# Gain and bias of the layer norm in two scalar_tensor_tensor operations on VectorE, and one weight load counted apart

## The reference, cut to what matters

```python
h = gelu(x @ W_down[role] + b_down[role])        # 512 -> 256
u = h @ W_up[role] + b_up[role]                  # 256 -> 512
y = x + u
mean = y.mean(-1); var = ((y - mean) ** 2).mean(-1)
out = (y - mean) * rsqrt(var + 1e-5) * gamma[role] + beta[role]
```

## Time and profile before

| | before |
|---|---|
| runs, us | 2103.6, 2101.53, 2102.2; median 2102.2 |
| profiled execution, us | 2103.55 |
| its span in the profile, us | 2101.8 |
| TensorE busy | 2080.2 us, 99% |
| VectorE busy | 1306.6 us, 62% |
| ScalarE busy | 921.1 us, 44% |
| GpSimd busy | 356.7 us, 17% |
| granted TensorE clock | 0.998 |

### The profile page before, as it was taken

How to read it: one execution, slowest core, us unless ns; L and a number is a source line. 1 busy time by engine, 2 the same in 40 slices (tenths; PEclk the granted TensorE clock), 3 DMA queues, 4 the chain that set the end, 5 groups by cost and what they waited for, 6 DMA issues and landing times.

```text
span 2101.8 us, 26697 instructions
## 1 busy us (share of the span) xinstructions
PE 2080.2 (99%) x9644; PEld 1719.8 (82%) x9644; DVE 1306.6 (62%) x2059; ACT 921.1 (44%) x1604; POOL 356.7 (17%) x344
## 2 busy tenths in 40 slices
PE   9999999999999999999999999999999999999997
PEld 7888888888788888888778888888878888888886
DVE  6576675546667667555667667555576766754566
ACT  5365444334356445334335544433334644533341
POOL 0011112210501101111040110112132111122104
PEclk9999999999999999999999999999999999999999
DMA  7411211122321121221450112111332012111232
GB/s 282 161 31 41 71 70 46 61 70 96 146 76 42 49 85 36 70 71 45 174 193 31 51 51 76 61 60 56 110 134 98 27 44 71 48 68 61 71 106 91
DMA packets 42368, 169.70 MB, mean 81 GB/s; under 512 B 5624, under 2 KB 9720, under 8 KB 34808
## 3 DMA queue, kind: packets, MB, share of 16 engines
q1 hardware_dynamic: 42096, 167.97, 23.2%
q10 hardware_dynamic: 144, 0.03, 0.0%
HBM read 146.97 MB, written 21.01 MB: 80 GB/s over the span
## 4 chain that ended last, share of the span: by engine, by line
PE 93%; DVE 3%; ACT 1%; issue 1%; POOL 1%; DMA 0%; SPq 0%; DVEq 0%; ACTq 0%; POOLq 0%
PE psum L581 85%; PE psum L836 2%; PE psum L873 1%; PE psum L656 1%; PE psum L678 1%; DVE acc L1446 0%; DVE fpart L1216 0%; PE psum L876 0%; DVE xs L1216 0%; ACT wup L1111 0%; PE psum L679 0%; PE psum L658 0%; DMA fraw<-fuse_in 0%; PE psum L861 0%; PE psum L849 0%
## 5 line engine op out<-in xcount | busy, mean ns | idle before, releaser
L581 PE MATMUL psum<-hs,wd 128*128 128x512 f32 x3072 | 718.0, 389 | 1.8 <-DVE acc L1446 1.8
L581 PEld LDWEIGHTS psum<-hs,wd 128*128 128x128 f32 x3072 | 576.0, 188 | 123.7 <-DVE acc L1446 3.4
L1446 DVE TENSOR_TENSOR acc<-psum,acc 128x512 f32<-128x512 f32 x448 | 294.3, 684 | 175.5 <-PE psum L581 174.3
L581 PE MATMUL psum<-cop,wsm 128*128 128x512 f32 x1416 | 354.7, 389 | 0.0
L581 PE MATMUL psum<-aop,wsm 128*128 128x512 f32 x1320 | 333.0, 389 | 0.0
L581 PE MATMUL psum<-aop,wsc 128*128 128x512 f32 x1320 | 311.3, 389 | 0.0
L581 PEld LDWEIGHTS psum<-cop,wsm 128*128 128x128 f32 x1416 | 265.8, 188 | 55.2
L581 PEld LDWEIGHTS psum<-aop,wsm 128*128 128x128 f32 x1320 | 247.7, 188 | 51.4
L581 PEld LDWEIGHTS psum<-aop,wsc 128*128 128x128 f32 x1320 | 247.4, 188 | 51.4
L1073 ACT ACTIVATE hs<-psum,bias 128x512 fp32r<-128x512 f32 x144 | 98.1, 682 | 394.5 <-PE psum L581 394.4
L1216 DVE TENSOR_TENSOR hs<-zt,hs 128x512 fp32r<-128x512 f32 x256 | 180.2, 704 | 125.7 <-ACT zt L1074 125.7
(11 more groups left out here) (168 smaller groups left out, 2372.1 us busy)
## 6 DMA issues: line engine op xcount, KB each, us to landing
w1m<-m_in SPq DMA_DIRECT2D x32, 1024.0 KB, 4.9
w1c<-c_in SPq DMA_DIRECT2D x32, 512.0 KB, 3.5
w<-c_in SPq DMA_DIRECT2D x32, 512.0 KB, 3.6
w<-m_in SPq DMA_DIRECT2D x32, 512.0 KB, 3.5
gains<-roles_in SPq DMA_DIRECT2D x30, 512.0 KB, 4.0
fw<-fused SPq DMA_DIRECT2D x6, 2048.0 KB, 10.4
fused<-fw SPq DMA_DIRECT2D x4, 2048.0 KB, 7.5
xmid<-x SPq DMA_DIRECT2D x4, 2048.0 KB, 6.7
```

The lines of the kernel that those rows point to most:

```text
L581: mm = nc.tensor.matmul(out, lhs(a), rhs(b), start=(start and n == 0), stop=(stop and n == total - 1), skip_group_check=reopened)
L1446: nc.vector.tensor_tensor(dst, d_out[o][:, :], dst, ALU.add).then_inc(acc_done, 1)
```

## The change

`BY_POOL` is new and 0, so the branches for i < BY_POOL do nothing here. GpSimd keeps the root alone, one per tile, in order. VectorE's `normalise(i)` becomes two scalar_tensor_tensor operations for each of the 32 tiles: (u - mean) * gain, which needs the gains and the mean, and then y * rstd + bias, which needs the root and the first one's end. The semaphore `e_done` of the second replaces `b_done` everywhere. The separate two operations for the last tile go. At the start, the first of the two loads of weight n = 2 counts on a semaphore of its own, and ScalarE may round the first input before the second has landed.

```diff
--- before.py
+++ after.py
@@ -62,6 +62,7 @@
 STRASSEN = UNITS - 2
 
 RANKED = 37
+BY_POOL = 0
 
 BASE, KB = 16512, 1024
 
@@ -197,6 +198,7 @@
         x_loaded = [sem(f"x_loaded{b}") for b in range(NTB)]
         chunk_loaded = [sem(f"chunk_loaded{k}") for k in range(KC)]
         fuse_loaded = {n: sem(f"fuse_loaded{n}") for n in range(1, 2 * LAYERS)}
+        third_loaded = sem("third_loaded")
         fuse_hi, fuse_lo, fuse_mm = sem("fuse_hi"), sem("fuse_lo"), sem("fuse_mm")
         fused_hi, fused_lo = sem("fused_hi"), sem("fused_lo")
         fuse_stored = [sem(f"fuse_stored{w}") for w in range(2)]
@@ -235,7 +237,7 @@
         gen_zeroed, xc_done, xz_hi, xz_lo = (sem(n) for n in ("gen_zeroed", "xc_done", "xz_hi", "xz_lo"))
         tr_done, dp_done, hg_done = (sem(n) for n in ("tr_done", "dp_done", "hg_done"))
         th_done, hz_hi, hz_lo, up_done = (sem(n) for n in ("th_done", "hz_hi", "hz_lo", "up_done"))
-        end_loaded, end_scaled, end_done = sem("end_loaded"), sem("end_scaled"), sem("end_done")
+        end_loaded, e_done = sem("end_loaded"), sem("e_done")
         st_done, ve_done, rstd_done = (sem(n) for n in ("st_done", "ve_done", "rstd_done"))
         yn_done, g_done, b_done = sem("yn_done"), sem("g_done"), sem("b_done")
         gb_loaded = [sem(f"gb_loaded{s}") for s in range(2)]
@@ -291,6 +293,12 @@
         def the_end(p, i):
 
             return p == PASSES - 1 and i == TILES - 1
+
+        def scaled(p, i):
+
+            if i >= BY_POOL:
+                return e_done, (TILES - BY_POOL) * p + i - BY_POOL + 1
+            return b_done, BY_POOL * p + i + 1
 
         def gain_loads(p, i):
 
@@ -341,7 +349,7 @@
                 if n >= 2:
                     sp.wait_ge(fuse_lo, fuse_n(n - 2))
                     for o in range(2):
-                        sp.dma_start(fuse_raw[n % 2][o], fuse_in[n, o]).then_inc(fuse_loaded[n], 16)
+                        sp.dma_start(fuse_raw[n % 2][o], fuse_in[n, o]).then_inc(third_loaded if (n, o) == (2, 0) else fuse_loaded[n], 16)
                 if n == 1:
                     sp.dma_start(bias[:, :, :], bias_in).then_inc(consts_in, 16)
                     sp.dma_start(rows_raw[:, :], rows_in).then_inc(brow_loaded, 16)
@@ -405,14 +413,11 @@
 
                 def load_gb(i):
                     if i >= 2:
-                        sp.wait_ge(b_done, 8 * p + i - 1)
+                        sp.wait_ge(*scaled(p, i - 2))
                     load_gains(half, layer, i)
 
                 def store(i):
-                    if the_end(p, i):
-                        sp.wait_ge(end_done, 2)
-                    else:
-                        sp.wait_ge(b_done, 8 * p + i + 1)
+                    sp.wait_ge(*scaled(p, i))
                     for b in range(2):
                         sp.dma_start(out[bass.ds(where[2 * i + b], 1)].rearrange("o t v -> (o t) v"),
                                      yt[b * SEQ:(b + 1) * SEQ, i % 4, :]).then_inc(stored[i % 4], 16)
@@ -547,23 +552,16 @@
                         pool.wait_ge(dn_done, 8 * UNITS * (p + 1))
                         nc.gpsimd.memset(xzg[:, :, :, 1, :].rearrange("p l k t -> p (l k) t").bitcast(F32), 0.0).then_inc(gen_zeroed, 1)
                         nc.gpsimd.memset(hzg[:, :, :, 1, :].rearrange("p l k t -> p (l k) t").bitcast(F32), 0.0).then_inc(gen_zeroed, 1)
-                    def root(i):
+                    for i in range(TILES):
                         e, s = 8 * p + i, i % 2
                         pool.wait_ge(ve_done, e + 1)
                         nc.gpsimd.tensor_tensor(rstd[:, s, :], veps[:, s, :], mhalf[:, :], ALU.pow).then_inc(rstd_done, 1)
-
-                    for i in range(TILES):
-                        e, s = 8 * p + i, i % 2
-                        if the_end(p, i):
-                            break
-                        root(i)
-                        if the_end(p, i + 1):
-                            root(i + 1)
-                        pool.wait_ge(gb_loaded[s], 16 * gain_loads(p, i))
-                        pool.wait_ge(yn_done, e + 1)
-                        nc.gpsimd.tensor_tensor(y[i % 4], y[i % 4], gains[:, s, 0:V], ALU.mult).then_inc(g_done, 1)
-                        pool.wait_ge(g_done, e + 1)
-                        nc.gpsimd.tensor_tensor(y[i % 4], y[i % 4], gains[:, s, V:2 * V], ALU.add).then_inc(b_done, 1)
+                        if i < BY_POOL:
+                            pool.wait_ge(gb_loaded[s], 16 * gain_loads(p, i))
+                            pool.wait_ge(yn_done, e + 1)
+                            nc.gpsimd.tensor_tensor(y[i % 4], y[i % 4], gains[:, s, 0:V], ALU.mult).then_inc(g_done, 1)
+                            pool.wait_ge(g_done, BY_POOL * p + i + 1)
+                            nc.gpsimd.tensor_tensor(y[i % 4], y[i % 4], gains[:, s, V:2 * V], ALU.add).then_inc(b_done, 1)
                     if layer == 1:
                         for s in range(4):
                             pool.wait_ge(stored[s], 32 * (TILES // 4) * (half + 1))
@@ -878,7 +876,7 @@
                 mm.then_inc(up_done, 1)
 
             def turn_back(p, half, i):
-                pe.wait_ge(b_done, 8 * p + i + 1)
+                pe.wait_ge(*scaled(p, i))
                 if 2 <= i < TILES - 3 or i == TILES - 1:
                     pe.wait_ge(x_back, 8 * half + i - 1)
                 for k in range(KC):
@@ -919,8 +917,11 @@
                             nc.scalar.activation(fuse_parts[n][o][:, HI, cols], fuse_raw[n][o][:, cols], ACT.Copy).then_inc(fuse_hi, 1)
                     return
                 act.wait_ge(fuse_mm, KC * (n - 1))
-                act.wait_ge(fuse_loaded[n], 32)
                 for o in range(2):
+                    if n == 2:
+                        act.wait_ge((third_loaded, fuse_loaded[n])[o], 16)
+                    else:
+                        act.wait_ge(fuse_loaded[n], 32)
                     nc.scalar.activation(fuse_parts[n % 2][o][:, HI, :], fuse_raw[n % 2][o], ACT.Copy).then_inc(fuse_hi, 1)
 
             def results(n):
@@ -1585,8 +1586,19 @@
                                 dve.wait_ge(tb_done, 8 * half + i - 3)
                             else:
                                 dve.wait_ge(stored[i % 4], 32 * (2 * half + i // 4))
+                        if i < BY_POOL:
+                            dve.wait_ge(rstd_done, 8 * p + i + 1)
+                            nc.vector.tensor_scalar(y[i % 4], u_bank[i % 3][:, :], mv[:, s, 0:1], rstd[:, s, :], ALU.subtract, ALU.mult).then_inc(yn_done, 1)
+                            return
+                        scale = gains_end[:, :] if the_end(p, i) else gains[:, s, :]
+                        dve.wait_ge(*((end_loaded, 32) if the_end(p, i) else (gb_loaded[s], 16 * gain_loads(p, i))))
+                        dve.wait_ge(st_done, 16 * p + 2 * i + 2)
+                        nc.vector.scalar_tensor_tensor(out=y[i % 4], in0=u_bank[i % 3][:, :], scalar=mv[:, s, 0:1], in1=scale[:, 0:V],
+                                                       op0=ALU.subtract, op1=ALU.mult).then_inc(yn_done, 1)
+                        dve.wait_ge(yn_done, 8 * p + i + 1)
                         dve.wait_ge(rstd_done, 8 * p + i + 1)
-                        nc.vector.tensor_scalar(y[i % 4], u_bank[i % 3][:, :], mv[:, s, 0:1], rstd[:, s, :], ALU.subtract, ALU.mult).then_inc(yn_done, 1)
+                        nc.vector.scalar_tensor_tensor(out=y[i % 4], in0=y[i % 4], scalar=rstd[:, s, :], in1=scale[:, V:2 * V],
+                                                       op0=ALU.mult, op1=ALU.add).then_inc(e_done, 1)
 
                     last = UNITS - 1
                     add(p, layer, last, 0, *range(KC))
@@ -1624,12 +1636,6 @@
                                 split_block(p + 1, 0, k)
                     row_stats(TILES - 1)
                     normalise(TILES - 1)
-            dve.wait_ge(end_loaded, 32)
-            dve.wait_ge(yn_done, TILES * PASSES)
-            yl = y[(TILES - 1) % 4]
-            nc.vector.tensor_tensor(yl, yl, gains_end[:, 0:V], ALU.mult).then_inc(end_scaled, 1)
-            dve.wait_ge(end_scaled, 1)
-            nc.vector.tensor_tensor(yl, yl, gains_end[:, V:2 * V], ALU.add).then_inc(end_done, 2)
 
 
 def _chunks(w):
```

## The result

The changed kernel takes 2095.17 us (median of 6 runs, 2094.39 to 2095.86), the kernel before 2102.9 beside it (6 runs, 2101.53 to 2105.15). The ratio is 0.9961, with an interval of 0.995 to 0.9972. In the profiled executions, 2103.55 became 2094.39 and the span 2101.8 became 2092.6.

What follows compares the result with a forecast made beforehand. TensorE was taken as the bound, busy 2080.2 of 2101.8 us. Gains of 4.85 + 2.6 + 0 = 7.45, say 7.5, took the median from 2102.2 to 2094.7 us; range 2092.8 to 2097.8.

Steps and rivals of the forecast that it cites:

- The end: End of the last pass: the last tile's stores begin at 2093.53 instead of 2098.38, a gain of 4.85 us.
- The price of the operations: In each tile: both new scalar_tensor_tensor operations on VectorE take 0.75 us each.
- The low bound: Price of the second new operation, both inputs in SBUF: 0.75 us taken, with 1.56 as the upper bound.
- The chained starts: On VectorE: 0.85 us from the first new operation to the second, 0.68 from the second to the next independent operation.
- VectorE's step: Tile stage: a full VectorE step becomes 4.75 us, against TensorE's 4.54 in layer 1 and about 5.0 in layer 0.
- the 3.95: Tile stage before the change: a full VectorE step without GpSimd beside it, 1046.18 - 1041.54 - 0.69 of waiting.
- The margin: Tile stage: tile 7's xz is ready 1.1 us before TensorE comes to it, so VectorE's lag costs 0.
- The pass ends: Pass ends: TensorE's waits for xs, the turn_back's biases and hz go, a gain of 2.6 us.
- the term 1.7 + 0.7 + 0.2: Pass ends: TensorE's listed waits, 1.7 us for xs, 0.7 for biases ahead of a turn_back, 0.2 for hz, all gained.
- wants one every 0.85: End of pass 1: TensorE wants one xs low part every 0.85 us, VectorE needs 0.62 each; no wait longer than 0.1.
- The gains: Gain loads VectorE now waits for: cost 0, with 1.2 us in hand at tile 5 of pass 1.
- The load apart: Start: counting the first load of weight n = 2 apart is worth 0, hidden by place_batches; at most 0.92 us otherwise.

Runs made afterwards that it cites:

- experiment 2: The kernel before, with VectorE scaling the tiles in the last pass alone and GpSimd those of the other passes; load apart included; 2099.08 us.
- Experiment 3: VectorE scales the tiles in the first three passes alone; the last pass is as in the kernel before; 2099.9 us.
- experiment 4: The changed kernel with two spare 128x512 multiplications on GpSimd behind the root of tile 5 in passes 0 and 1; 2098.82 us.
- Experiment 6: The changed kernel with BY_POOL = 6: GpSimd scales tiles 0 to 5 of each pass, VectorE tiles 6 and 7; 2099.86 us.
- Experiment 5: The changed kernel with the first scalar_tensor_tensor of every tile made twice on VectorE; 2102.51 us.
- 7: The changed kernel with place_batches moved behind operands(2) and results(0), and SyncE's store of that result ahead of its wait for the ranks; 2090.03 us.
- 8: The kernel of 7 with the two loads of weight n = 2 counted together again; 2090.63 us.
- experiment 1: The kernel before with only the first load of weight n = 2 counted apart; 2103.98 us, ratio 1.0005.
- experiment 9: The kernel of 7 with a wait put back in front of TensorE's matmuls of weight n = 2; 2094.24 us.
- 10: The kernel of 7 with the second of the last tile's two stores issued by ScalarE; 2089.87 us.
- 11: The kernel of 7 with BY_POOL = 4: GpSimd scales tiles 0 to 3 of each pass, VectorE tiles 4 to 7; 2091.68 us.

## Why the prediction held, step by step

- *The end, 4.85.* Right in size and in its parts: the stretch is 4.92 shorter. The last VectorE operation ends 3.20 after the start of TensorE's last matmul, where the forecast had 2093.49 - 2090.26 = 3.23, and the stores begin 0.03 after it. Experiments 2 and 3 show that this part depends on the last pass alone.
- *The price of the operations, 0.75 each.* Measured 0.748 and 0.752. The low bound was the right choice, and experiment 4 shows what the high one comes from: beside GpSimd the second operation takes 1.44. Experiment 6 has the counterpart: the first operation, which has one of its inputs in PSUM, ran wholly beside a multiplication of GpSimd (2090.84 to 2091.59, within 2090.64 to 2091.92) and kept its 0.75. The Trainium skill (SBUF — State Buffer, "Who interferes with whom") has this as a rule on VectorE operations with two SBUF inputs; experiment 4 agrees with it.
- *The chained starts, 0.85 and 0.68.* The first was mis-sized: 0.78 to 0.79 passes from the first to the second (2087.64 to 2088.43). I had taken the room behind an operation of 0.81 from one row. The second measured 0.67.
- *VectorE's step, 4.75.* Measured 4.58 to 4.60 (4.66 for the first step of pass 1). Of the difference of some 0.16, 0.07 is the term above. The rest lies in the 3.95, from which a listed wait of 0.69 was taken. Ahead of that bn_stats the hz row starts at 1045.08, and where bn_stats does not wait it starts 0.33 after the start of hz (1055.08 to 1055.41). It came at 1046.18, so the wait cost 0.77: 4.64 - 0.77 + 0.78 + 0.67 - 0.72 = 4.60. The margin held and no wait for xz was added (1.2 in 4, as before). Experiment 5 puts the point where it breaks: with 0.78 more, the passes lose 5.6.
- *The pass ends, 2.6.* The mechanism was right: the waits for all three go, and xs takes 2.49. The size was short: 3.83. The step that failed is the term 1.7 + 0.7 + 0.2, read from the list of waits. In that list a wait begins where the last matmul ends by the trace. But a matmul's row at the end of a series is longer than its share of a series. In the earlier trace rows three matmuls of xs last 0.94 and are followed by 0.66 of waiting, so the next three start 1.59 later; after the change 48 of them take 11.16, or 0.70 for three. The listed 0.66 cost 0.89. By the same reckoning the other listed wait there, 0.72, cost 0.99. These two alone are 0.50 above the list. The others went the same way. At the end of pass 0 the third wait for xs is listed with 0.31 and cost 0.53 (six matmuls from 562.89, the next at 564.85, where six take 1.43 after). The turn_back's transposes of yt start 1.33 behind those of xct before (557.13 to 558.46) and 0.44 after (556.67 to 557.11), so the 0.73 cost 0.89. The transposes behind the 0.22 for hz start 0.72 behind the matmul ahead of them before (1063.81 to 1064.53) and 0.43 after, so 0.29. Together 0.89 + 0.99 + 0.53 + 0.89 + 0.29 = 3.59 of the 3.83. The prediction's "wants one every 0.85" has the same error: TensorE wants a low part every 0.70, which a low part of 0.62 still meets. Experiment 3, in which the three waits went and nothing else that TensorE feels, gained 3.74 in the passes.
- *The gains, 0.* Right in effect. Their landing took 4.7 in place of the 4.0 of the earlier trace rows, and tile 7 of pass 1 waited 0.25 for them, behind everything that TensorE needed.
- *The load apart, 0.* Right, and experiments 7 and 8 show that place_batches was the cover. Without it the load apart gave 0.6, within the prediction's bound of 0.92.
- *The total.* The forecast was 2094.7, the median 2095.17. This is nearer than the terms deserve, and in part luck: the stretches of the passes and the end sum to 8.75 where I had 7.45, while the medians differ by 7.7 (2102.9 - 2095.17). The medians of before lay between 2102.2 and 2103.8, depending on the runs. In the profiles it is the start that differs, 530.86 to 534.40 in kernels whose start has the same pause, while passes and end repeat within 0.1.

## What to carry to other kernels

Work given to a second engine to relieve a first can cost more than it takes: the 30 added VectorE operations (2089 in place of 2059) cost TensorE nothing, and the 62 removed GpSimd ones gave 3.8 us in the passes. Two causes are in that. The waits for xs, 2.4 us, come with both engines reading SBUF side by side, which by itself brings such waits back in experiment 4. Those for the turn_back and for hz, 1.2 us, come by the traces from the queue on GpSimd, where a tile took two operations and a root stood behind them. Cut two traces at instructions that both have before comparing medians, since a stretch agreed within some 0.1 us where the runs spread over 4. And count a wait from the starts of the rows around it, not by the idle time that is listed.

## What was not expected of the hardware

A pause of TensorE can cost more than its length, and not the same in each execution. Windows over TensorE's pause at 29 to 32 us, of the kernel after, of experiment 1 and of experiment 2. The columns are the window, its length, TensorE's busy time with its instructions, the granted clock as a share of 2.4 GHz, the DMA share and GB/s.

```profile
24.00:29.00 5.00, 5.00 (x23) 1.00 0.84 347
29.00:33.00 4.00, 1.06 (x3) 0.83 0.46 128
33.00:36.00 3.00, 3.00 (x10) 0.66 0.42 118
36.00:40.00 4.00, 4.00 (x20) 1.00 0.89 370
```

```profile
29.00:33.00 4.00, 1.26 (x6) 0.93 0.43 123
33.00:36.00 3.00, 2.73 (x7) 0.50 0.41 116
36.00:40.00 4.00, 4.00 (x12) 0.59 0.72 273
40.00:44.00 4.00, 4.00 (x19) 1.00 0.98 353
```

```profile
29.00:33.00 4.00, 0.91 (x5) 1.00 0.41 114
33.00:36.00 3.00, 3.00 (x15) 1.00 0.36 113
36.00:40.00 4.00, 4.00 (x19) 1.00 0.87 350
```

In front of the pause, from 24 to 29 us, the granted clock is 1.00 in all profiles. Behind it, it is at the lower level (0.50, 1.2 GHz) for part of the time in all profiled executions of kernels that have the pause but two, experiments 2 and 9; it stays at 1.00 in the four kernels without the pause. The Trainium skill (TensorE: Matmul & The Clock Gate, Part 1, "The HAM clock gate") has these two levels of the clock.

What that costs is read from the 96 matmuls behind the pause. They take 22.03 us in experiment 2, where the clock stayed, 23.40 in the kernel after, 24.80 in 6 and 24.84 in 1: up to 2.8 more. The start of experiment 1 is 534.40 where that of 2 is 530.86, 3.5 more; 2.8 of this are those matmuls, and 0.7 is that TensorE came out of the pause later (33.27 against 32.55), having waited 1.00 for fpart earlier.

This fits what the medians did. The kernels with the pause spread over 1.5 to 4 us between runs (5 to 33 runs each), those without it (7, 8, 10 and 11, five runs each) over 0.2 to 0.9; 9, with the pause and five runs, over 1.7. Taking the pause out gave 5.1 us in the median, for a listed wait of 2.9. The mean granted clock of each run points the same way: in experiment 4 it is 1.000 for the two fastest runs (2096.14 and 2096.63) and 0.998 for the six slowest (2098.82 to 2100.19), and in 6 it is 0.999 for the five fastest and 0.998 for the six others. In 9 it is 0.999 for all five, too coarse for a spread of 1.7 us. So that the slower runs of experiment 9 had the lower clock is inferred, and not shown.
